# Prologue of a fused adaLN, attention and FFN kernel: another order of the weight loads, the constants and the first splits

## The reference, cut to what matters

```python
h  = einsum('bct,bcd->bdt', x, cond_weights[subject]) + bias[subject]
q, k, v = h @ Wq.T, h @ Wk.T, h @ Wv.T                       # 16 heads of 32
p  = softmax(q k / sqrt(32) + alibi_causal)                  # 64 x 64 a head
x  = x + (p v) @ Wo.T
g  = einsum('bct,bcd->bdt', x, cond2_weights[condition])
u  = square(relu(act_quant(fwht(g)) @ ternary(w_up).T))      # 512 -> 1024
x  = x + act_quant(fwht(u)) @ ternary(w_down).T
```

## Time and profile before

| | before |
|---|---|
| median of 3 runs | 749.63 us (748.5 to 751.21) |
| span of the profiled execution, first to last instruction | 746.9 us |
| PE busy | 720.9 us, 97% |
| DVE busy | 667.8 us, 89% |
| ACT busy | 418.9 us, 56% |
| POOL busy | 208.7 us, 28% |
| mean granted TensorE clock | 0.995 of full |

### The profile page before, as it was taken

The page is one execution under the profiler, slowest core; times in us unless marked ns, Lnnn a source line. Parts: engine busy times, 40 slices in busy tenths (PEclk is TensorE's granted clock), DMA queues, the critical chain, the costliest instruction groups (busy, mean ns, idle before and its releaser), DMA issues.

```text
span 746.9 us, 23704 instructions
## 1 busy us (share of the span) xinstructions
PE 720.9 (97%) x9904; PEld 612.7 (82%) x9936; DVE 667.8 (89%) x1349; ACT 418.9 (56%) x842; POOL 208.7 (28%) x223
## 2 busy tenths in 40 slices
PE   8898899999999999999999999999999999998787
PEld 5787798888888888888898888888888888886563
DVE  3797999999999999999999999999999999889977
ACT  2477556555565565565656555565565565654431
POOL 1231433322233332223333322333332223331100
PEclk9999999999999999999999999999999999999999
DMA  7742111111111110111111011111110101000100
GB/s 241 246 142 65 36 51 51 29 37 40 50 52 51 52 47 21 36 51 52 51 51 51 22 43 40 51 52 52 51 46 24 65 16 32 18 31 2 32 31 29
DMA packets 37567, 39.94 MB, mean 53 GB/s; under 512 B 21204, under 2 KB 21588, under 8 KB 37460
## 3 DMA queue, kind: packets, MB, share of 16 engines
q1 hardware_dynamic: 34324, 32.04, 14.0%
q10 hardware_dynamic: 3136, 6.39, 2.5%
HBM read 30.02 MB, written 8.39 MB: 51 GB/s over the span
## 4 chain that ended last, share of the span: by engine, by line
PE 82%; DVE 11%; ACT 2%; issue 1%; DMA 1%; POOL 1%; SPq 1%; ACTq 0%; DVEq 0%
PE bank L394 43%; PE bank L546 8%; PE bank L587 6%; PE bank L420 4%; PE bank L384 4%; PE bank L528 4%; PE bank L555 4%; PE bank L466 3%; PE bank L483 3%; DVE hid L286 2%; PE bank L536 1%; PE bank L571 1%; DVE hid_max L1112 1%; POOL gT L286 1%; DVE hid L1100 1%
## 5 line engine op out<-in xcount | busy, mean ns | idle before, releaser
L286 POOL TENSOR_TENSOR gT<-gT 128x256 f32<-128x256 f32 x116 | 98.7, 871 | 418.8 <-ACT gT L803 416.5
L286 DVE TENSOR_TENSOR hid<-hid 128x512 f32<-128x512 f32 (+1 forms) x130 | 99.5, 807 | 0.2
L778 ACT ACTIVATE v_kd<-bank 64x256 f32<-64x256 f32 x128 | 48.5, 379 | 74.4 <-PE bank L394 73.3
L1422 POOL TENSOR_TENSOR s<-s,srow 128x512 f32<-128x512 f32 x64 | 67.5, 1058 | 39.1 <-DVE srow L1036 39.1
L394 PE MATMUL bank<-h_hi,wq_hi 128*128 128x256 f32 x256 | 75.4, 295 | 2.5 <-DVE wq_lo L972 2.5
L394 PE MATMUL bank<-h_hi,wk_hi 128*128 128x256 f32 x252 | 73.4, 291 | 0.0
L394 PE MATMUL bank<-h_hi,wq_lo 128*128 128x256 f32 x256 | 73.0, 285 | 0.0
L394 PE MATMUL bank<-h_lo,wq_hi 128*128 128x256 f32 x256 | 72.9, 285 | 0.0
L394 PE MATMUL bank<-h_hi,wk_lo 128*128 128x256 f32 x252 | 71.1, 282 | 0.0
L394 PE MATMUL bank<-h_lo,wk_hi 128*128 128x256 f32 x252 | 71.1, 282 | 0.0
L814 ACT ACTIVATE late<-bank 128x512 f32<-128x512 f32 x64 | 37.7, 589 | 52.5 <-PE bank L546 52.5
(11 more groups left out here) (146 smaller groups left out, 1938.1 us busy)
## 6 DMA issues: line engine op xcount, KB each, us to landing
x_in<-in_x_dram SPq DMA_DIRECT2D x32, 256.0 KB, 2.6
x_res<-in_x_dram SPq DMA_DIRECT2D x32, 256.0 KB, 3.3
out_dram<-late SPq DMA_DIRECT2D x31, 256.0 KB, 3.4
w_in<-in_L_cond_weights_dram SPq DMA_DIRECT2D x126, 16.0 KB, 2.4
bias_in<-in_fside_8xS_dram SPq DMA_DIRECT2D x62, 32.0 KB, 3.2
k_bd<-in_L_attn_Wk_dram ACTq DMA_DIRECT2D x1, 1024.0 KB, 5.5
s<-in_L_attn_Wq_dram ACTq DMA_DIRECT2D x1, 1024.0 KB, 7.7
v_kd<-in_L_attn_Wv_dram ACTq DMA_DIRECT2D x1, 1024.0 KB, 12.2
```

What stands on the lines that cost most here:

```text
L286: eng.tensor_tensor(dv[:, :, n], sv[:, :, 0], sv[:, :, 1], op).then_inc(done, 1)
L778: ins = act.activation(v_kd[b * T:b * T + T, c % 4, e], blocks[e * T:e * T + T, :, b, :], ACT.Copy)
L1422: pool.tensor_tensor(s[:, c % 2, hs, :], s[:, c % 2, hs, :], srow[:, 2, hs].unsqueeze(2).broadcast_to([P, 8, T]), ALU.mult).then_inc(p_pn, 1)
```

## The change

On SP conditions 2 and 3 are asked for before the position bias pT. On ACT wq is asked for as before; wv is asked for behind the two copies of h; the two halves of wq are split directly behind that, each followed by one of the first two job copies; the up weights and wo are asked for behind those. Further down each half of wv is split one job copy later. Nothing is added or removed, and the programs of PE, DVE and POOL are the same.

```diff
@@ SP
             sp.dma_start(cst_sb[:, H * T:], cst[:, H * T:]).then_inc(s_cst, 16)
+            for c in range(2, 4):
+                load_cond1(c, c - 1)
             sp.dma_start(flat(pT), cst[:, 0:H * T]).then_inc(s_alibi, 16)
-            for c in range(2, 6):
+            for c in range(4, 6):
                 load_cond1(c, c - 1)
@@ ACT
             load_w("wq", wqT)
-            load_w("wv", wvT)
             copy_hi(0)
             copy_hi(1)
+            load_w("wv", wvT)
+            split_w("wq", 0, 2)
+            copy_qk(1, 0, 0, bank[2])
+            split_w("wq", 2, 4)
+            copy_qk(2, 0, 1, bank[3])
             load_ffn_weight(act, 0, 0)
-            copy_qk(1, 0, 0, bank[2])
             load_ffn_weight(act, 0, 1)
-            copy_qk(2, 0, 1, bank[3])
+            copy_qk(3, 0, 2, bank[2])
             load_w("wo", woT)
-            split_w("wq", 0, 2)
-            split_w("wq", 2, 4)
-            copy_qk(3, 0, 2, bank[2])
             copy_qk(4, 0, 3, bank[3])
             act.wait_ge(s_mask, 1)
             act.wait_ge(s_wlo, 1)
             spread_k(0)
+            copy_qk(5, 0, 4, bank[2])
             split_w("wv", 0, 2)
-            copy_qk(5, 0, 4, bank[2])
+            copy_qk(6, 0, 5, bank[3])
             split_w("wv", 2, 4)
-            copy_qk(6, 0, 5, bank[3])
             copy_qk(7, 0, 6, bank[2])
             copy_hi(2)
             copy_qk(8, 0, 7, bank[3])
```

## The result

The changed kernel takes 751.31 us in the median of 20 runs (748.23 to 755.41), the kernel before 749.36 (20 runs, 746.4 to 751.91): a ratio of 1.0027, 95% interval 1.0015 to 1.0039. It is slower by some 2 us, and lies 0.3 us above the top of the range forecast. Over both the mean is 750.9 (32 runs) against 749.7 for the kernel before on three chips (101 runs).

The account below looks back on a forecast made before the run. Early waits from wq's split through DVE's and ACT's fixed orders to the scores were taken to bind, beside PE at 97% busy; 746.9 us span less 1.0, plus 2.7 to the median, gave 748.6, range 746.8 to 751.0.

Parts of the forecast that it names:

- When wq lands: Load of wq: with pT behind conditions 2 and 3, its split on ACT starts at 15.7 us instead of 17.59.
- PE beside it: PE's jobs: job 2 waits 1.0 us for copy 1; job 4 starts near 20.0 us, not 21.45.
- ACT's queue behind the split: ACT from the split's start T: second wv_lo at T + 8.8, queue longer by 0.84 us, wv_lo 1.05 earlier.
- The pause ahead of the scores: PE before the scores: idle for 2.3 us, as DVE's and ACT's order sets the scores at 29.5.
- rival (a): Scores on PE: the new pause brings the half clock, 1.5 us lost, 749.9, no change; chance 0.27.
- The sum: Whole run: 746.9 us of span less 1.0 is 745.9; with 2.7 between span and median, 748.6.
- Rival (b): DVE's absolute sum: up half 0 lands late, gain gone after 26.6 us, up to 754.9; chance 0.07.
- Rival (c): Load of wq: no earlier if wv made it late, T stays 17.35; 0.6 us slower, 750.2; chance 0.09.
- The range: Whole run's time: 746.8 to 751.0 us, meant to include the spread of the runs.

Follow-up runs that it names:

- e1: The changed kernel with 11 dummy matmuls in PE's pause between condition 3 and the scores of pair 0; mean 749.4 us, ratio 0.9995 to the kernel before.
- e2: The changed kernel with ACT's last job copy ahead of copy_hi(2) instead of behind it; mean 749.3 us, ratio 0.9989 to the kernel before.
- e7: The changed kernel with DVE's bias of condition 2 ahead of the absolute sum over the up weights; median 746.4 us, ratio 0.9961 to the kernel before.
- e4: The changed kernel with SP's order of before, so ACT's part of the change alone; mean 751.4 us, ratio 1.0026 to the kernel before.
- e3: The kernel before with SP's part of the change alone, conditions 2 and 3 ahead of the position bias; mean 749.9 us, ratio 1.0000.
- e5: The changed kernel with wo's three DMAs issued behind both halves of wv's split; mean 749.6 us, ratio 0.9997 to the kernel before.
- e12: The changed kernel unaltered, timed again beside the kernel before as its second series; median 750.19 against 749.28 us, ratio 1.0008.

## Why the prediction was wrong, step by step

- **When wq lands** was right: 6.05 us from request to split forecast, 5.38 in the first profile, 6.86 in the second, and 5.5 to 5.7 in the other kernels in which both loads stand as changed or pT stands between conditions 2 and 3. By the table pT had been most of the cause, with a scatter of its own (6.8 once without it).
- **PE beside it** was right: job 4 forecast near 20.0 without a pause, and it started at 20.05. Job 2 waited 0.36 us for copy 1 and not 1.0, since job 1 had itself ended 0.7 later than forecast. (wv's landing, given as 19.5, comes to 19.2 by the figures beside it; nothing hangs on it.)
- **ACT's queue behind the split** was mis-sized, and this is one of two steps that failed. T + 8.8 forecast for the second wv_lo; it started at 25.47 (24.25 and one piece of 1.22), T + 9.8. The term is wo's issues, 2.3 us (0.40 and 1.87) where I took 1.5 from the earlier trace rows. The gain at the bias of condition 2, 1.0 forecast, was 0.78 by the profile although wq came 0.7 sooner than I took. From the split to the scores the changed kernel needs 14.79, 14.31 and 14.77 us in three profiles (first, second, e1) and the kernel before 12.99: longer by 1.3 to 1.8 where 0.84 was forecast (0.82 by the forecast's own 8.8 and 7.98). So the gain at the scores, 1.05 forecast, was 0.78, -0.22 and 0.61 counted from wq's request.
- **The pause ahead of the scores** was right: 2.3 forecast, 2.58 twice measured; so was what sets it, DVE's and ACT's order (e2, e7).
- **The choice between the forecast and rival (a)** is the other step that failed. I gave the half clock 0.27 and left it out of the likeliest sum. Its price was right (1.5 for the stretch; 1.43 by the profile, and in e1's profile it is gone), but it is no either-or of the kernel: it falls in some executions and not in others. The trace of before had shown one such execution, and its price there was already part of 749.6. The new pause should have gone into the sum with its share, as the old one stood in the median. That share is not known; by the fit all the half clock that the changed kernel has more is worth 0.76 us a run. The length of a pause does not tell either: the 1.75 us pause at 684 that stood as a sign without half clock is followed by it in the changed kernel (0.72 above).
- **Both together do not reach the miss.** A gain of 1.0 was forecast and a loss of 1.3 measured in the means, 2.3 apart: 0.76 go to the clock by the fit, some 0.6 to the queue by these three profiles against one of before, and the rest, some 0.9, is open.
- **The sum** took the 2.7 us between span and median as lying outside the profiled instructions. Every run on record is 1.7 to 1.9 us longer than its span, so the rest of the 2.7 is that the profiled execution was some 0.9 us faster than the median of its three. The 748.6 is the median less 1.0 all the same.
- **Rival (b)** did not happen: up half 0 landed 1.4 us before it was wanted (1.3 forecast). The position bias was forecast at 26.2 and landed at 29.2, without cost here, and it was the next limit in e7.
- **Rival (c)** was wrong for its reason: not a late wq but a longer queue eats the gain. That its 750.2 is the second series' median is luck; the first is 1.1 above it.
- **The range** took the spread of three runs; the 20 of each kernel spread over 5.5 and 7.2 us.

What stays open: why the changed kernel has more half clock in its first series (12.3 us a run) than in the second (9.7), and the 0.50 us at equal half-clock time. By the same fit e4 is 1.35 us slower than before at equal half-clock time, e1 0.93 and e3 0.68 slower, e5 0.24 faster (standard error 0.25 each). e4 and e5 point to ACT's part and to wo's issues within it, but e3, which has ACT's order of before, shows that the fit leaves differences of this size between kernels that have no such cause. Whether the half clock fell on the scores in a timed run is not seen, only in the profiled ones.

## What to carry to other kernels

Before the head of a chain is moved forward, follow the engine queues behind it to the next instruction that stands in a fixed order: here the gain at wq's split (2.6 us in one profile, 1.1 in the other) met five DMA issues on ACT and a 2.3 us reduction on DVE, and with one line moved on DVE on top (e7) the kernel became faster than before, which the change alone did not make it. A pause of TensorE that is moved may take a half clock along, so its price belongs to the new place, weighed by how often the half clock falls. And where runs differ by their half-clock time, a kernel is compared by many runs with that time beside them, not by two profiles.

## What the runs showed of the hardware that I had not expected

- The same pause of PE at the same place is followed by the half clock in one execution and not in another: 2.58 us ahead of the scores (changed kernel yes, e12 no), 1.15 and 1.27 us close to each other in step 2 (e12 yes, before no), 1.75 us near 685 (changed kernel yes, before no).
- A DMA issue on ACT is no fixed 0.5 us: the two gT issues took between 0.97 and 1.87 us in these kernels, and hold everything behind them on that engine.
- The same 1 MB load in the same place took 5.4 and 6.8 us to land in two executions (wq, changed kernel), and the inputs of the first conditions let wq be asked for anywhere between 9.5 and 10.8 us.
